# A DLRM tower on one core: tables' high parts placed in PSUM, casts further ahead, and a new order of a group's work

## The reference

```
e = stack([tbl_f[ids[:, f]] for f in range(26)], axis=1)
combined = concatenate([dense_features[:, None, :], e], axis=1)     # 2048 x 27 x 128
interactions = einsum('bnd,bmd->bnm', combined, combined)           # the 351 pairs above the diagonal
h = concatenate([dense_features, pairs, dense_features], axis=1)
h = maximum(h @ W_top1 + b_top1, 0)                                 # 607 -> 512
h = maximum(h @ W_top2 + b_top2, 0)                                 # 512 -> 256
y = h @ W_top3                                                      # 256 -> 1
```

## Time and profile before

| | us |
|---|---|
| median of 3 runs | 384.82 |
| lowest and highest | 381.84, 385.08 |
| the profiled execution, its own time | 385.81 |
| span of its instructions | 383.9 |
| busy: PE, DVE, ACT, POOL | 333.5, 260.9, 169.3, 269.4 |

### The profile page before, as it was taken

One profiled execution on the slowest core, in us unless ns is written; L12 is line 12 of the kernel. 1 busy time (PEld: TensorE's weight loads), 2 busy tenths in 40 slices (PEclk: granted clock), 3 DMA queues, 4 the chain that ended last, 5 costly groups with the idle time before them and its releaser, 6 DMA issues.

```text
span 383.9 us, 13545 instructions
## 1 busy us (share of the span) xinstructions
PE 333.5 (87%) x6208; PEld 303.5 (79%) x6208; DVE 260.9 (68%) x206; ACT 169.3 (44%) x248; POOL 269.4 (70%) x277
## 2 busy tenths in 40 slices
PE   3777895949899998999899989999898989969787
PEld 2656784939898897979898879889897889859676
DVE  3999889574849865787668775777666776723322
ACT  2553563514445443545364543544354434532412
POOL 6787777777777777777777777777777777776000
PEclk9999998797999999999999999999999999997999
DMA  7996124251224322242215221341224112332020
GB/s 181 234 236 188 51 70 112 57 158 50 56 55 118 88 58 56 66 144 52 56 51 158 51 57 54 94 121 50 56 66 143 51 50 58 97 99 56 2 92 0
DMA packets 18985, 33.51 MB, mean 87 GB/s; under 512 B 5834, under 2 KB 11666, under 8 KB 18930
## 3 DMA queue, kind: packets, MB, share of 16 engines
q0 software_dynamic: 8848, 18.11, 18.2%
q1 hardware_dynamic: 10082, 14.55, 13.5%
HBM read 28.96 MB, written 3.68 MB: 85 GB/s over the span
## 4 chain that ended last, share of the span: by engine, by line
PE 40%; POOL 34%; issue 13%; DVE 7%; DMA 3%; ACT 2%; DVEq 0%; SPq 0%
POOL rows L390 34%; PE gram_ps L714 8%; PE hot_ps L684 8%; PE mlp_ps L684 8%; PE mlp_ps L720 4%; DVE one_hot L538 3%; PE transpose_ps L650 3%; PE mlp_ps L721 3%; PE mlp_ps L722 3%; DVE units L527 2%; DMA rows<-table,ids_sb 1%; PE hot_ids_ps L659 1%; PE mlp_ps L761 1%; DMA rows<-bounce 1%; DVE packed_lo L549 1%
## 5 line engine op out<-in xcount | busy, mean ns | idle before, releaser
L390 POOL DMA_INDIRECT rows<-table,ids_sb x272 | 268.5, 987 | 83.5 <-issue 80.7
L538 DVE TENSOR_TENSOR one_hot<-hot_ids_ps,row_numbers_sb 125x2048 fp32r<-125x2048 f32 x72 | 165.2, 2298 | 72.2 <-PE hot_ids_ps L659 62.7
L684 PE MATMUL hot_ps<-one_hot,table_hi 125*128 125x256 f32 x320 | 82.5, 295 | 3.4 <-issue 2.9
L684 PE MATMUL hot_ps<-one_hot,table_lo 125*128 125x256 f32 x320 | 79.6, 286 | 0.0
L684 PE MATMUL mlp_ps<-one_hot,table_hi 125*128 125x256 f32 x256 | 66.6, 297 | 11.8 <-DVE hidden_lo L569 6.4
L684 PEld LDWEIGHTS hot_ps<-one_hot,table_hi 125*128 125x128 f32 x320 | 62.1, 194 | 4.6 <-issue 4.6
L714 PE MATMUL gram_ps<-embed_t 128*27 128x27 f32 x4096 | 54.9, 195 | 11.2 <-issue 4.8
L684 PE MATMUL mlp_ps<-one_hot,table_lo 125*128 125x256 f32 x256 | 63.8, 286 | 0.0
L714 PEld LDWEIGHTS gram_ps<-embed_t 128*27 128x27 f32 x4096 | 45.0, 106 | 23.0 <-issue 15.4
L684 PEld LDWEIGHTS hot_ps<-one_hot,table_lo 125*128 125x128 f32 x320 | 62.3, 195 | 0.1
L684 PEld LDWEIGHTS mlp_ps<-one_hot,table_hi 125*128 125x128 f32 x256 | 49.9, 195 | 14.6 <-DVE one_hot L538 7.4
(11 more groups left out here) (80 smaller groups left out, 381.4 us busy)
## 6 DMA issues: line engine op xcount, KB each, us to landing
rows<-table,ids_sb POOLq DMA_INDIRECT x272
embed_t<-table SPq DMA_DIRECT2D x8, 448.0 KB
bounce<-units SPq DMA_DIRECT2D x8, 448.0 KB, 2.6
scratch<-bounce SPq DMA_DIRECT2D x7, 378.0 KB
dense_sb<-dense_t SPq DMA_DIRECT2D x8, 128.0 KB
scratch<-w SPq DMA_DIRECT2D x1, 512.0 KB, 4.8
units<-w_units SPq DMA_DIRECT2D x2, 252.0 KB
scratch<-table SPq DMA_DIRECT2D x1, 448.0 KB
```

Source lines behind the costliest of these rows:

```text
L390: nc.gpsimd.indirect_dma_start(rows[:, t2, f - 1, :], None, tables[table], bass.IndirectOffsetOnAxis(ids_sb[:, tile, table:table + 1], 0)) ...
L538: nc.vector.tensor_tensor(one_hot[:, k % RING], ids.to_broadcast([HOT_P, HOT_STEPS, GROUP]), row_numbers_sb[:, :, None].to_broadcast([HOT_ ...
L684: last = nc.tensor.matmul(hot_bank(n), table[:, n, step, :], one_hot[:, k % RING, step, :], start=(step == 0 and table is table_hi), stop= ...
```

## The change

Three things are changed. First, a table's low part: PE multiplies the identity (now cast whole, 128 columns, in place of a selector of 36) with the cast table, two products of 512 columns into both banks of `gram_ps` (`place_hi`), and DVE subtracts the PSUM banks from the raw table. `place_hi(k)` waits for the cast and for the subtraction of table k-1; `place_hi(0)` stands ahead of the eight warming products, and `place_hi(n + 1)` ahead of look-up n. The clearing of `gram_ps` is dropped. Second, ACT casts one table further ahead, and the ids of the hot tables are loaded to 64 partitions, with the other 64 set to zero by DVE. Third, `STEPS` has a new order, for PE, ACT and DVE.

```
 STEPS = [
-    "G0 S0 Q0 H0 M0 Q1 Q2 H1 G1 W0 Q3 H2 W1 M1 Q4 M2 W2 H3 W3".split(),
-    "G0 M3 Q0 H4 W4 M4 D0 E0 Q1 Q2 H5 W5 G1 Q3 H6 M5 Q4 H7 H8 M6".split(),
+    "G0 S0 Q0 H0 W0 H1 G1 Q1 W1 M0 M1 Q2 M2 H2 W2 Q3 H3 W3 Q4 M3 H4".split(),
+    "G0 Q0 H5 W4 M4 M5 G1 Q1 E0 Q2 H6 W5 H7 Q3 H8 Q4 D0 M6".split(),
 ]
...
-        selector = sb("selector", [P, PAIR_ROWS], F32R)
+        identity_r = sb("identity_r", [P, P], F32R)
...
+        def in_banks(table):
+            return table.rearrange("p (a j) d -> p a (j d)", a=2)
...
-            nc.gpsimd.dma_start(hot_ids_sb[:, :], hot_ids).then_inc(hot_ids_loaded, 16)
+            nc.gpsimd.dma_start(hot_ids_sb[0:HOT_IDS_P, :], hot_ids).then_inc(hot_ids_loaded, 16)
...
             split_hi(0)
+            split_hi(1)
             for step, n in [(x[0], int(x[1:])) for x in FIRST_STEPS]:
                 if step == "H":
-                    if n + 1 < HOT:
-                        split_hi(n + 1)
+                    if n + 2 < HOT:
+                        split_hi(n + 2)
                     hot_copy(0, n, 0)
...
             def split_lo(k):
-                dve.wait_ge(hi_split, k + 1)
-                lower(raw_tables[k], table_hi[:, k], table_lo[:, k]).then_inc(lo_split, 1)
+                dve.wait_ge(hi_placed, k + 1)
+                nc.vector.tensor_tensor(in_banks(table_lo[:, k]), in_banks(raw_tables[k]), gram_ps[0:HOT_P, :, :],
+                                        ALU.subtract).then_inc(lo_split, 1)
...
-            nc.vector.memset(gram_ps[:, :, :], 0.0).then_inc(banks_zeroed, 1)
+            nc.vector.memset(hot_ids_sb[HOT_IDS_P:P, :].bitcast(F32), 0.0).then_inc(rest_zeroed, 1)
...
-            nc.vector.tensor_copy(selector[:, :], identity_sb[:, 0:PAIR_ROWS]).then_inc(selector_ready, 1)
+            nc.vector.tensor_copy(identity_r[:, :], identity_sb[:, :]).then_inc(selector_ready, 1)
...
+            def place_hi(k):
+                pe.wait_ge(hi_split, k + 1)
+                if k >= 1:
+                    pe.wait_ge(lo_split, k)
+                for a in range(2):
+                    last = nc.tensor.matmul(gram_ps[:, a, :], identity_r[0:HOT_P, :], in_banks(table_hi[:, k])[:, a, :],
+                                            start=True, stop=True)
+                last.then_inc(hi_placed, 1)
...
+            pe.wait_ge(rest_zeroed, 1)
             broadcast_ids(0)
+            place_hi(0)
...
                 if step == "H":
+                    if n + 1 < HOT:
+                        place_hi(n + 1)
                     look_up(0, n)
...
-            pe.wait_ge(banks_zeroed, 1)
             group(0, 0, STEPS, first=True)
```

More of the change, by code:

```diff
@@ L68 @@
 PAIR_ROWS = HOT * GROUPS // PAIR
+HOT_IDS_P = 64
 HALF = N // 2
@@ L198, in dlrm_tower @@
         selector_ready = sem("selector_ready")
+        rest_zeroed = sem("rest_zeroed")
         hot_ids_ready = sem("hot_ids_ready")
@@ L202, in dlrm_tower @@
         hot_copied = sem("hot_copied")
-        banks_zeroed = sem("banks_zeroed")
+        hi_placed = sem("hi_placed")
         weights_hi = sem("weights_hi")
@@ L659, in broadcast_ids @@
                 nc.tensor.matmul(hot_ids_ps[0:HOT_P, :],
-                                 selector[:, pair:pair + 1].to_broadcast([P, HOT_P]), hot_ids_sb[:, :],
+                                 identity_r[:, pair:pair + 1].to_broadcast([P, HOT_P]), hot_ids_sb[:, :],
                                  start=True, stop=True).then_inc(hot_ids_ready, 1)
+            def place_hi(k):
[6 more added lines that the diff above has]
+                last.then_inc(hi_placed, 1)
             def look_up(g, n):
@@ L828, in _ @@
             pe.wait_ge(hot_ids_loaded, 16)
+            pe.wait_ge(rest_zeroed, 1)
             broadcast_ids(0)
+            place_hi(0)
             for _ in range(FIRST_WARM_PRODUCTS):
-                nc.tensor.matmul(transpose_ps[0:HOT_P, 0].rearrange("p i d -> p (i d)"), selector[:, 0:1].to_broadcast([P, HOT_P]),
+                nc.tensor.matmul(transpose_ps[0:HOT_P, 0].rearrange("p i d -> p (i d)"), identity_r[:, 0:1].to_broadcast([P, HOT_P]),
                                  hot_ids_sb[:, :], start=True, stop=True)
@@ L890 @@
         late[:, k:k + HALF, k - 1] = 1
-    hot_ids = np.zeros((P, PAIR * GROUP), np.int32)
+    hot_ids = np.zeros((HOT_IDS_P, PAIR * GROUP), np.int32)
     hot_ids[:PAIR_ROWS] = a["ids"].T[HOT_TABLES].reshape(HOT, GROUPS, GROUP).transpose(1, 0, 2).reshape(PAIR_ROWS, PAIR * GROUP)
```

## The result

The changed kernel takes 415.19 us (median of 4 runs, 411.32 to 420.03), the kernel before 384.73 (4 runs): ratio 1.077, 95% interval 1.067 to 1.087. The profiled execution took 413.43 us with a span of 411.6, against a forecast of 413.8 and 411.9.

A forecast was written before the change was run, and what follows sets the result against it. POOL's gathers were taken to bound the kernel before, TensorE second. Group 1's start 82.0 + 6 passes of 48.35 = 372.1, + 13.3 + 26.5 = 411.9 span, + 1.9 = 413.8 us; range 390 to 422.

The forecast's parts named there:

- Rival 1: SyncE's queue: the units' store isn't late, POOL and PE keep their old paces; 379.4 us, chance 0.11.
- Rival 2: Start of a pass: the store is late but only M0 waits; pass 43.5 us, time 383.7, chance 0.06.
- rival 3: TensorE's clock stays low for more than one stretch a pass; 51 us a pass, 429 us, chance 0.08.
- M0's wait: PE in each pass: waits 1.7 us at M0 for the late units.
- DVE's stand: DVE stands at S0 for the late units, two one-hots queued behind; PE then waits 3.8 us at M2.
- The pass: Each pass, new order: 15.75 + 24.4 + 6.2 = 46.35 us, with the clock loss 48.35.
- the round trip of the units: Behind dense's low part: store to second issue 2.65 us, landing 3.45, units' low part done at d+8.75.
- The clock: TensorE at half clock after two waits in every pass: 2.0 us a pass, bounds 0 and 2.9.
- Group 1: Its first Gram product starts at 82.0 us instead of 83.02, group 0 taking about 36.8.
- The last group: From G0 to the last transposes: M0's wait of 1.75 and the low clock go, 17.7 become 13.3 us.
- The tail: After the last transposes: 26.5 us, which the change doesn't touch.
- POOL: Eight gathers no longer held under table subtractions: 5.0 us back, last gather issued at 348.9.

The follow-up runs named there:

- experiment 3: Changed kernel, store still late, with S0 (high and low part of the units) moved from behind G0 to directly ahead of M0: 405.73 us, ratio 1.050.
- experiment 4: Changed kernel, store still late, with 24 filler products on TensorE (168 in all) ahead of M0's wait for the units: 423.04 us, ratio 1.095.
- experiment 5: Changed kernel with the units' store ahead of the dense load, table low parts again subtracted from the SBUF copy instead of PSUM: 389.85 us, ratio 1.012.
- tail_swap: Changed kernel with units' stores ahead of the dense load, and the last units' store ahead of group 6's y store: 380.54 us, ratio 0.987.

## Why the prediction was right

**The mechanism, shown.** D0 at the pass's end delays the dense load, and the store queued behind it, though it needs neither; one line moved in the queue gives 33 us back, and the order alone costs 27.5. Rivals 1 and 2 fall with that, rival 3 too (one stretch of half clock a pass, none over 6.8 us). Rival 2's own price was wrong besides. Its condition, DVE not standing at S0, is experiment 3: 43.5 us a pass were given for it, 47.0 measured. M0's wait had been put at 1.7 and is 3.1 to 4.3 there, and the half clock behind it had been left out. So DVE's stand, which the prediction had as the longer of two waits, is worth 0.8 us a pass; the late units alone make most of the loss.

**The pass.** In pass 3, from d, the end of dense's low part (177.57), to M2 the text has 15.75 us, the trace 16.26; from M2 to the next d, 30.6 against 30.7. Inside, the round trip of the units was too short: store to second issue 3.67 instead of 2.65, landing 3.74 instead of 3.45, so the low part ends at d+9.7, not 8.75; DVE's queue behind it took 6.55 instead of 7.0.

**The clock, a term that hit for a wrong reason.** The text adds 2.0 us a pass for half clock. It came once a pass, as said. In pass 3 it came behind M0's wait and was hidden under M2's: that wait was 0.80 instead of 3.8 because slow products filled it, and with the clock whole (experiment 4) the stretch was no shorter. Pass 3 closes at 47.0 without the term. Counted from d to d the others up to pass 5 are longer: pass 1 by 1.0, with the units 1.0 later; passes 2 and 4, with the wait at the ids product, by 1.7 and 1.3; pass 5 by 0.7, with its half clock behind M2, where TensorE is busy. Waits of one engine and its half clock had been added where one lies inside the other, and the wait at the ids product wasn't in the text at all.

**Terms that cancelled.** Group 1 started at 78.91, not 82.0: the constants landed 1.8 us earlier, the first placing pair was at 7.65 and the first look-up ended at 14.6 instead of 15.9; group 0 took 35.8 instead of 36.8. Six passes together were 3.1 short. The last group took 14.4 instead of 13.3, since M0 still waits 1.73. The reason given for that wait to go, that pack(6) has no dense load ahead of it, holds for the kernel before too, where its store is issued 6.4 us ahead of the group's first Gram product (333.38 against 339.74) and M0 waits 1.75 all the same. The tail took 31.3 instead of 26.5: -3.1 - 3.1 + 1.1 + 4.8 = -0.3. That the span came out within 0.3 us is luck; that the time lay in the range is not. The largest failed step is "the tail, which the change doesn't touch". It isn't edited, but M6 shifted against the units' store: in the kernel before, M6 ends first; in this one the store of the last units waits for the y store (392.09, the units complete at 389.16) and the round takes 4.5 us instead of 2.5. The order has no part in it: with the order alone the tail takes 26.3 us, and what delays M6, a gap of 2.74 in "issue", is not ahead of it there.

**POOL.** Gain 5.0 predicted, 6.3 (tables only) and 6.7 (experiment 5) measured. Rival 1's 379.4 for a store in time was 3 to 4 us too low (382.2 and 383.3), the tail again: it had the last transposes at 352.0, and they came at 348.7.

## What to carry to other kernels

SyncE's in-order queue makes every entry wait for the conditions of those ahead. When a step is moved in a schedule, write down for each queue what stands behind each wait that the step releases; here one entry's place in the queue was worth 33 us, and the order of the compute, with the queue put right, about 1. Don't add an engine's waits and its lost clock before asking whether a second engine sets the later meeting point anyway. And a stretch that the change doesn't touch keeps its length only while the arrivals in it keep their order.

## What the hardware showed besides

On the chips that take 385 us, TensorE's long gaps in "issue" go with how far it is in its instructions, not with a time or a kind of work. In the six kernels with the same 18 products more than before (changed, store undelayed, tables only, S0 late, the y store behind, the SBUF subtraction) 1.7 to 2.7 us are lost ahead of TensorE's 6,111th recorded instruction, M6's first, at times from 358 to 390. With 26 more products ahead of M6 the gap lies in the same place of the count, inside G1, and is 0.56; with the 168 products of experiment 4 it is 1.78 ahead of the 6,112th. In the kernel before and in the order-only one they are ahead of the 973rd (2.35, 2.45) and the 5,610th (1.37, 1.29). So added instructions shift such a gap onto other work. What causes it was not settled.

The store of the units to its second issue took 2.48 us in some tails (tail_swap, and before: 366.26 to 368.74) and 3.9 to 4.8 in others, and not only behind a y store (3.87 in tail_swap's kernel with the filler, with none ahead); in two kernels it took 2.5 us behind a y store. What sets it is open.

One chip ran the four kernels that were also run elsewhere 29 to 44% slower, the kernel before by 42% (546.8 us), with a part of TensorE's time lost in "issue"; on it an edit that costs 7% elsewhere gained 3%. A comparison holds for the balance of engines on which it was made.
